# Final sums of a graph layer with routed experts: all early tiles stored first and then added in four transfers, with the GpSimd queue listed anew

## What is computed

```python
x = x + gnn(layernorm(x), src, dst, W, b)            # gather by src, sum by dst, @W, relu
logits = layernorm(x) @ Wr + br
top_p, top_idx = top_k(softmax(logits), 2)
weights = top_p / top_p.sum()
xe = layernorm(x) * ln_g[e] + ln_b[e]
y_e = gelu(xe @ W1[e] + b1[e]) @ W2[e] + b2[e]       # D=256, H=1024
out = x + weights[0] * y_{first} + weights[1] * y_{second}
```

## Time and profile before

| what | value |
|---|---|
| median of three runs | 1662.73 us (1662.26 to 1664.24) |
| the profiled execution's own time | 1661.44 us |
| span of its trace | 1660.0 us |
| TensorE busy | 1192.6 us (72%) |
| VectorE busy | 952.5 us (57%) |
| ScalarE busy | 595.0 us (36%) |
| GpSimd busy | 1116.0 us (67%) |
| mean granted TensorE clock | 0.82 of full |

### The profile page before, as it was taken

How to read it: one execution, slowest core, us unless ns; L and a number is a source line. 1 busy time by engine, 2 the same in 40 slices (tenths; PEclk the granted TensorE clock), 3 DMA queues, 4 the chain that set the end, 5 groups by cost and what they waited for, 6 DMA issues and landing times.

```text
span 1660.0 us, 26618 instructions
## 1 busy us (share of the span) xinstructions
PE 1192.6 (72%) x9098; PEld 989.6 (60%) x9098; DVE 952.5 (57%) x2502; ACT 595.0 (36%) x1169; POOL 1116.0 (67%) x1115
## 2 busy tenths in 40 slices
PE   6954565647358645995599659969839858689995
PEld 5954344535146314982488439848728747479984
DVE  8997456656434353656264734764645749466552
ACT  4954011111032004440345025516315335356662
POOL 5006777777777777777777777777777757673333
PEclk9999566666578557996699769979959969799998
DMA  6027866675375447974787469759658578999882
GB/s 187 1 98 266 266 219 203 213 232 179 117 260 163 110 119 261 312 222 129 260 270 253 138 217 316 255 192 305 188 189 292 179 252 265 258 294 305 264 251 51
DMA packets 195546, 354.75 MB, mean 214 GB/s; under 512 B 25572, under 2 KB 93446, under 8 KB 195412
## 3 DMA queue, kind: packets, MB, share of 16 engines
q1 hardware_dynamic: 130120, 205.39, 36.6%
q0 software_dynamic: 58928, 141.26, 29.5%
q10 hardware_dynamic: 6364, 6.40, 1.2%
HBM read 290.80 MB, written 64.07 MB: 214 GB/s over the span
## 4 chain that ended last, share of the span: by engine, by line
PE 35%; DMA 25%; POOL 19%; issue 9%; DVE 8%; ACT 3%; SPq 0%; POOLq 0%; DVEq 0%; ACTq 0%
DMA gt<-zt,srcI 12%; POOL gt L832 9%; PE ps L1251 9%; PE ps L1266 9%; PE ps L1165 8%; DMA out<-gt,toks 6%; POOL xs L861 6%; DMA out<-acc 3%; PE ps L1140 2%; POOL out L891 2%; PE ps L1176 2%; DVE ohl L1340 2%; PE ps L1203 2%; DMA xb<-xs 1%; ACT h L1112 1%
## 5 line engine op out<-in xcount | busy, mean ns | idle before, releaser
L832 POOL DMA_INDIRECT gt<-zt,srcI x832 | 834.1, 1003 | 254.2 <-issue 181.6
L1165 PE MATMUL ps<-gt,S 128*128 128x257 f16 x1664 | 345.7, 331 | 200.3 <-DMA gt<-zt,srcI 198.9
L1165 PEld LDWEIGHTS ps<-gt,S 128*128 128x128 f16 x1664 | 203.5, 152 | 298.2 <-DMA gt<-zt,srcI 282.8
L1251 PE MATMUL ps<-xe,w1b 128*128 128x256 f16 x2688 | 343.2, 282 | 36.0 <-DVE xe L1656 18.9
L1266 PE MATMUL ps<-w2b,hT 128*128 128x256 f16 x2688 | 315.5, 275 | 13.5 <-DVE yb L1688 7.7
L1251 PEld LDWEIGHTS ps<-xe,w1b 128*128 128x128 f16 x2688 | 269.9, 101 | 78.6 <-DVE xe L1656 21.6
L1112 ACT ACTIVATE h<-ps,cb 128x256 f32<-128x256 f32 x448 | 227.1, 557 | 241.4 <-PE ps L1251 236.4
L1662 DVE SCALAR_TENSOR_TENSOR hT<-h,cb,hT 128x512 f16<-128x512 f32 x224 | 167.7, 750 | 237.4 <-ACT hT L1116 236.8
L1266 PEld LDWEIGHTS ps<-w2b,hT 128*128 128x128 f16 x2688 | 264.3, 99 | 47.5 <-issue 15.4
L1116 ACT ACTIVATE hT<-h,cb 128x512 f16<-128x512 f32 x224 | 161.7, 722 | 7.3
L1090 ACT ACTIVATE aT<-ps 128x256 f32<-128x256 f32 x98 | 37.4, 381 | 314.7 <-PE ps L1196 314.6
(11 more groups left out here) (264 smaller groups left out, 1246.7 us busy)
## 6 DMA issues: line engine op xcount, KB each, us to landing
w1b<-ws SPq DMA_DIRECT2D x56, 1024.0 KB, 6.5
w2b<-ws SPq DMA_DIRECT2D x56, 1024.0 KB, 8.1
ws<-w2b SPq DMA_DIRECT2D x16, 1024.0 KB, 5.0
xb<-xs SPq DMA_DIRECT2D x56, 260.0 KB, 8.3
gt<-zt,srcI POOLq DMA_INDIRECT x832, 4.2
ys<-yb SPq DMA_DIRECT2D x34, 256.0 KB, 7.8
w1b<-in_L_ffn_W SPq DMA_DIRECT2D x8, 1024.0 KB, 8.7
hT<-in_L_ffn_W SPq DMA_DIRECT2D x8, 1024.0 KB, 13.9
```

The costliest lines, as they stand in the source:

```text
L832: e.indirect_dma_start(out=gt[:, i % NG, :], out_offset=None, in_=zt, in_offset=bass.IndirectOffsetOnAxis(ap=srcI[:, c, r:r + 1].bitcast(u ...
L1165: inst = e.matmul(PS[r % 2][:, 0:257], S[:, r % NS, :, c], gt[:, i % NG, part * 257:part * 257 + 257], start=(c == 0 and part == 0), stop= ...
L1251: inst = e.matmul(UP[n % 2][:, z * BS:(z + 1) * BS], w[:, l, kk, j * 128:(j + 1) * 128], xe[m % 2][:, k, kk, :], start=(kk == 0 and l == 0 ...
```

## The change

Tiles 0 to 9 are treated like the others: `nd2` stores their rows without the fetched ones (three more stores), their combine only weights, ten stores of finished tiles by SP go, and there are four `sums` in place of three (tiles 0-9, 10-19, 20-29, 30-40). A new semaphore `s_late` takes the two stores of the last chunk out of the first wait of the chain; the first give of the last chunk (block 38) waits for it. In the planner, the constants of POOL's steps change: a pair or a scatter is listed only when POOL is free within 0.3 us, and not just before a give or sums is due; a combine follows its pair after 6.0 us; a `sums` is booked with 2.0 us of POOL and holds the chain for 3.0 us and 1.1 us per tile; a `give` is booked with 3.7 us and holds the chain for 4.5 us.

```diff
-TP = 10
-NSUM = -(-(TG - TP) // 11)
-SUMS = [(TP + (TG - TP) * i // NSUM, TP + (TG - TP) * (i + 1) // NSUM) for i in range(NSUM)]
+NSUM = 4
+SUMS = [(TG * i // NSUM, TG * (i + 1) // NSUM) for i in range(NSUM)]
...
-        if max(s["chain"], s["plain"], s["base"]) > s["now"] or clock["POOL"] > s["now"] + 2.6:
+        if max(s["chain"], s["base"]) > s["now"] or clock["POOL"] > s["now"] + 0.5:
             return False
         if batches and batches[0][0] <= s["now"]:
             b = batches.popleft()[1]
-            emit("sums", b, (("POOL", 1.3 * (SUMS[b][1] - SUMS[b][0])),), s["now"])
+            emit("sums", b, (("POOL", 2.0),), s["now"])
+            s["chain"] = clock["POOL"] + 3.0 + 1.1 * (SUMS[b][1] - SUMS[b][0])
             s["summed"] += 1
-        elif gives:
-            emit("give", gives.popleft(), (("POOL", 3.4),), s["now"])
+        elif gives and (BLOCKS[gives[0]][0] < LAST or s["late"] <= s["now"]):
+            emit("give", gives.popleft(), (("POOL", 3.7),), s["now"])
+            s["chain"] = clock["POOL"] + 4.5
             s["given"] += 1
         else:
             return False
-        s["chain"] = clock["POOL"] + 5.0
         return True
...
-                if kind == "cg" and clock["POOL"] > s["now"] + 2.5:
+                if kind in ("cg", "xs") and (clock["POOL"] > s["now"] + 0.3 or (gives or batches) and s["now"] + 1.0 < max(s["chain"], s["base"]) + 1.0 < s["now"] + 2.0):
...
-                chain.at = end + 2.0 if kind == "cg" else s["now"] if kind == "xs" else end
+                chain.at = end + 6.0 if kind == "cg" else s["now"] if kind == "xs" else end
...
-        BASE_DMAS = sum(1 for c, a0, a1 in GROUPS if TP <= a0 < TG)
-        OUT_DMAS = sum(1 for c, a0, a1 in GROUPS if a0 >= TG) + (1 if GROUPS[-1][2] - 1 > GROUPS[-1][1] else 0)
+        BASE_DMAS = sum(1 for c, a0, a1 in GROUPS if a0 < TG)
+        OUT_DMAS = sum(1 for c, a0, a1 in GROUPS if a0 >= TG and c < LAST)
+        LATE_DMAS = sum(1 for c, a0, a1 in GROUPS if c == LAST) + (1 if GROUPS[-1][2] - 1 > GROUPS[-1][1] else 0)
...
                     e.wait_ge(s_out, 16 * OUT_DMAS)
-                    e.wait_ge(s_co, 16 * TP)
...
+                    if BLOCKS[m][0] == LAST > BLOCKS[m - 1][0]:
+                        e.wait_ge(s_late, 16 * LATE_DMAS)
...
-                elif kind == "nd2" and GROUPS[arg][1] >= TP:
+                elif kind == "nd2":
...
-                elif kind == "cc":
-                    t = arg
-                    if t < TP:
-                        e.wait_ge(s_comb, t + 1)
-                        e.dma_start(out[t * 128:(t + 1) * 128, :], row(t)).then_inc(s_co, 16)
...
-                    if t < TP:
-                        then(e.scalar_tensor_tensor(out=row(t), in0=fetched_rows(t, 0), scalar=wts[:, 0, t:t + 1], in1=row(t),
-                                                    op0=ALU.mult, op1=ALU.add))
-                    else:
-                        if t == TP:
-                            e.wait_ge(s_base, 16 * BASE_DMAS)
-                        then(e.tensor_scalar(row(t), fetched_rows(t, 0), wts[:, 0, t:t + 1], None, ALU.mult))
+                    if t == 0:
+                        e.wait_ge(s_base, 16 * BASE_DMAS)
+                    then(e.tensor_scalar(row(t), fetched_rows(t, 0), wts[:, 0, t:t + 1], None, ALU.mult))
```

More of the change, by code:

```diff
@@ L170, in plan @@
     clock = {"PE": 0.0, "DVE": 0.0, "ACT": 0.0, "POOL": 0.0}
-    s = {"now": 0.0, "bank": 0.0, "held": {}, "free": {}, "norms": -1, "nT": 0, "nW": 0, "hh": 0, "xr": 0, "placed": 0, "tabled": 0, "read": -1, "routed": -1, "loaded": 0, "asked": False, "given": 0, "plain": 1e9, "base": 1e9, "summed": 0, "chain": 0.0}
+    s = {"now": 0.0, "bank": 0.0, "held": {}, "free": {}, "norms": -1, "nT": 0, "nW": 0, "hh": 0, "xr": 0, "placed": 0, "tabled": 0, "read": -1, "routed": -1, "loaded": 0, "asked": False, "given": 0, "base": 1e9, "late": 1e9, "summed": 0, "chain": 0.0}
     later, sent = [], {}
@@ L395, in step_job @@
                     s["read"] = arg
-                if kind == "cc" and arg == TP - 1:
-                    s["plain"] = end + 4.0
                 if kind == "cc" and any(arg == b1 - 1 for b0, b1 in SUMS):
                     batches.append((end, [b1 - 1 for b0, b1 in SUMS].index(arg)))
-                if kind == "nd2" and arg == NGR - 1:
-                    s["base"] = end + 4.0
+                if kind == "nd2" and ends(arg) in (LAST - 1, LAST):
+                    s["base" if ends(arg) < LAST else "late"] = end + 4.0
                 if kind == "sent":
@@ L690, in gnn_ffn @@
         s_out = sem("s_out")
+        s_late = sem("s_late")
         s_xrow = sem("s_xrow")
@@ L720, in gnn_ffn @@
         s_comb = sem("s_comb")
-        s_co = sem("s_co")
         XS_BEFORE = [sum(2 * (t1 - t0) for t0, t1 in CHUNKS[:c]) for c in range(len(CHUNKS) + 1)]
-        BASE_DMAS = sum(1 for c, a0, a1 in GROUPS if TP <= a0 < TG)
-        OUT_DMAS = sum(1 for c, a0, a1 in GROUPS if a0 >= TG) + (1 if GROUPS[-1][2] - 1 > GROUPS[-1][1] else 0)
+        BASE_DMAS = sum(1 for c, a0, a1 in GROUPS if a0 < TG)
+        OUT_DMAS = sum(1 for c, a0, a1 in GROUPS if a0 >= TG and c < LAST)
+        LATE_DMAS = sum(1 for c, a0, a1 in GROUPS if c == LAST) + (1 if GROUPS[-1][2] - 1 > GROUPS[-1][1] else 0)
         NODE_T = {}
@@ L979, in sync @@
                         e.dma_start(out[a0 * 128:full * 128, :].rearrange("(t p) c -> p t c", p=128),
-                                    acc[:, a0:full, 0:256]).then_inc(s_base if a0 < TG else s_out, 16)
+                                    acc[:, a0:full, 0:256]).then_inc(s_base if a0 < TG else s_out if c < LAST else s_late, 16)
                     if full < a1:
-                        e.dma_start(out[48 * 128:N, :], acc[0:TAIL, T - 1, 0:256]).then_inc(s_out, 16)
-                elif kind == "cc":
-                    t = arg
-                    if t < TP:
-                        e.wait_ge(s_comb, t + 1)
-                        e.dma_start(out[t * 128:(t + 1) * 128, :], row(t)).then_inc(s_co, 16)
+                        e.dma_start(out[48 * 128:N, :], acc[0:TAIL, T - 1, 0:256]).then_inc(s_late, 16)
                 elif kind == "st":
```

## The result

| what | before | changed |
|---|---|---|
| median | 1664.06 us (1662.26 to 1671.19, 7 runs) | 1675.62 us (1672.99 to 1680.14, 7 runs) |
| the profiled execution's own time | 1661.44 us | 1677.33 us |
| span | 1660.0 us | 1675.8 us |
| first pair issued | 1348.94 us | 1353.77 us |
| from there to the end of the span | 311.1 us | 322.0 us |

The ratio is 1.0065 (95%: 1.0049 to 1.0081), so slower, and outside the range given. So times of it are compared after taking off 4.83 us, "in the clock of before". The loss of 11 us lies behind the first pair.

What follows compares the result with a forecast made beforehand. It took TensorE's waits behind in-order VectorE, and at the end POOL's transfer chain, to bound the last stage. TensorE 5.7 us later, chain wait 5.5 less, 0.1 rounding: no change, median 1662.8 us, range 1654 to 1671.

Steps and rivals of the forecast that it cites:

- From 1349 to 1402, the scatters: First pairs to scatters: waits at combines 0, 1 and 5 go; scatters run 1.5 us earlier, from 1404.8 to about 1415.6.
- The restart: Block 38 behind the scatters: starts near 1426.5 instead of 1432.38, 5.9 us gained.
- Combine 24: Behind the second sums: pair 24 lands with it at 1454.0; TensorE idles 8 us, `up` 40 is 2.9 us late.
- Combine 33: Behind the third sums: pair 33 lands at 1485.9, so `y` 40 ends at 1488.6, 5.7 us late.
- The tail: Kernel's end: the chain catches up with TensorE; `y` 55 at 1648.7 sets the end, give 55 at 1649.4.
- The predicted 5.5 us: Kernel's end: 5.5 us less waiting of give 55 for the chain, set against TensorE being 5.7 us later.
- the estimate of 5.0 us for a ten-tile sums: Skill's rule for a POOL transfer, about 2.0 us plus bytes over 436 GB/s; by it pair 24 would not wait.
- The slower one: Rival: sums land after 17.5 us instead of 13.6 each; `y` 40 13.5 us late, median 1670; chance 0.22.
- pairs issued right behind a full-size sums land after the 5.7 us of the others: Fast rival, at combines 24 and 33: `y` 40 ends 2 us early, median 1656; chance 0.32.

Runs made afterwards that it cites:

- f4: The kernel before with only its three sums booked at 2.0 us of POOL instead of 1.3 us a tile; ratio 1.0057, stretch 325.9 us.
- g1: The change with combines 24 and 25 moved directly ahead of 26, and 33 and 34 ahead of 35, in VectorE's order; ratio 0.9984, stretch 311.2 us.
- g4: The kernel before with only the planner's lag of a combine behind its pair set to 6 us instead of 2; ratio 1.0002, stretch 312.2 us.
- g3: The change with all four sums held until the last pair is issued; ratio 1.0140, stretch 339.3 us.

## Why the prediction was wrong

Its mechanism held: VectorE waits for pair 24 and pair 33, each landing with a sums, and TensorE behind it. What failed are the sizes: two landings that it put too short, and the later issues that follow from them, moved the sum by 11 us. By its steps, in the clock of before:

- *From 1349 to 1402, the scatters.* Right. No combine up to 5 waits over 0.6 us; scatters 1405.9 to 1416.5, predicted 1404.8 to 1415.6.
- *The restart.* Right: 1425.1 for 1426.5, a gain of 7.3 us for 5.9.
- *Combine 24.* **The first failing step: the second sums was put at 1439.7 and went at 1444.8.** The text let it follow pair 23 at once. But it is in the chain and has to wait for give 37. With the 6.8 us that the prediction used for a give, give 37, issued up to 1434 and so with its second transfer from about 1432, would have landed by 1439 and held nothing. In fact that transfer went at 1434.6 (the scatters ended 1 us later, and give 37 waited 1.93 us for give 36, 7.93 us to land) and **landed after 9.31 us, not 6.8**, at 1443.9. A nearer figure was in the trace of before: give 35, right behind its scatters, landed after 8.7 us. The landing of the sums, 13.7 us for the predicted 13.6, was right, and so was pair 24 landing with it. `up` 40 came at 1462.0, predicted 1456.4; TensorE's wait was 11.25 us for the 8 of the text (8.8 by its own times). The front part has a slip here too: pair 24 moved behind two more gives, not one, and one more sums, as its lists show.
- *Combine 33.* The third sums went at 1477.7 instead of 1471.6: the 5.1 us were handed on by way of `y` 38, for which give 38 waited 4.04 us, and **its landing took 17.5 us, not 13.6**. Pair 33 landed at 1496.6 for 1485.9, and `y` 40 ended at 1499.65 (1503.73 and 0.75, less 4.83) for 1488.6. These are the 11 us: 6.1 of a later issue, 3.9 of a longer landing, 1.0 between.
- *The tail.* Right: the chain caught up and `y` 55 set the end, finished at 1660.0 for 1648.7, and what follows give 55 took 10.1 us for 10.7. The predicted 5.5 us came and went into the 16.7 us by which `y` 40 was late.
- *By the Trainium skill*, "DMA: Bandwidth & Descriptors", section "Anatomy of one DMA — SWDGE (gpsimd) path", the estimate of 5.0 us for a ten-tile sums is contradicted again: 11.5 to 17.5 us for the changed kernel's three. For one tile its rule makes an estimate of 2.3 us; the run with one tile showed 3.1 to 4.3.
- *The rivals.* The slower one, the sums taking longer, had the right direction and place (1670 us), but only in part the right price. It had `y` 40 13.5 us late, and 16.7 were measured; of the 11.0 beyond the forecast's 5.7 a longer landing of a sums gave 3.9, the rest came with the later issues. That pairs issued right behind a full-size sums land after the 5.7 us of the others did not occur in any trace of the 1665 us sittings: they took 8.2 us and more.

What the prediction did not see is what the runs add. The cost hangs on where the combines stand in VectorE's list against the landing of their pairs: with POOL's order unchanged, combines listed early cost 0.57% (f4), and the change with four combines later costs nothing (g1). And two limits lie close together at the end of this kernel, the blocks' products up to `y` 55 and POOL's chain of gives and sums. Where give 55 waited for the chain, that came 5.5 us behind what `y` 55 allowed in the kernel before, 0.4 in g1 and 13.6 in g4 (1648.60 less 1634.25, where `y` 55 is finished, and 0.77). The kernel before, g1 and g4 are ended by the chain, so a gain at the restart brings nothing there. The change is ended by `y` 55: VectorE's waits push that 17.0 us back (309.7 for 292.6), and what goes beyond the chain is the loss.

## What to carry over

A transfer's booked time in a planner does two jobs: how long the queue is busy with it, and how soon what is queued behind it can be used. Setting it to the 2 us of issue is right for the first and wrong for the second. When an engine works in order, price a step not by whether its operand is late but by what is listed behind it, and in a chain of transfers add every link's own landing before the next issue. And before counting a gain, find the second limit of the end: here it was 5.5 us away.

## What was not expected of the hardware

- An accumulating transfer of ten or eleven tiles landed after 10.7 to 20.4 us over the runs of the usual sittings (11.5 to 19.7 in the two traces of the changed kernel), one of a single tile after 3.1 to 4.3 us. The four in a row of g3, with no pair or give between them, were no faster (16.7 to 19.9), so the pairs and gives between are not what makes such a landing long. What makes it vary is not shown.
- In the stretch with its waits of 11 us TensorE was granted less clock: 0.87 over the 90 us with both, 0.94 in the same stretch of g1 and 0.98 in the kernel before. The 24 matmuls right behind the two waits took 4.66 and 4.50 us, others 2.78.
- The same kernel took 1665 us in three sittings and 1944 and 1916 us in two, for a cause that the traces do not show, and in the first of these two the verdict on this change turned round (0.9940).
